# Another order of work in the projections of an attention and fp4 feed-forward layer

## The reference

```python
q, k, v = (split_heads(einsum('bsh,oh->bso', x, w) * s + b) for w, s, b in ...)   # 16 heads of 16
attn = softmax(einsum('bhqd,bhkd->bhqk', q, k) / 4)
x = layernorm(x + (einsum('bhqk,bhkd->bhqd', attn, v) -> [b,s,256]) @ w_o.T * s_o + b_o)
gate, y = fp4(x) @ fp4(w_gate).T, fp4(x) @ fp4(w_up).T       # 704 wide
h = silu(gate) * y
out = layernorm(x + fp4(h) @ fp4(w_down).T)
```

## Time and profile before

| | |
|---|---|
| median of 3 runs | 2128.46 us |
| profiled execution, own time | 2129.26 us |
| its span | 2127.5 us |
| TensorE / VectorE / ScalarE / GpSimd busy | 96% / 89% / 79% / 38% |
| projections (0 to 233 us): TensorE / VectorE / ScalarE busy | 198.9 / 145.1 / 125.8 us |
| attention (233 to 1560 us): TensorE / VectorE / ScalarE busy | 1291.1 / 1231.3 / 1150.0 us |
| feed-forward (1560 to 2128 us): TensorE / VectorE / ScalarE busy | 554.6 / 524.1 / 396.9 us |

### The profile page before, as it was taken

One profiled execution on the slowest core, in us unless ns is written; L12 is line 12 of the kernel. 1 busy time (PEld: TensorE's weight loads), 2 busy tenths in 40 slices (PEclk: granted clock), 3 DMA queues, 4 the chain that ended last, 5 costly groups with the idle time before them and its releaser, 6 DMA issues.

```text
span 2127.5 us, 42069 instructions
## 1 busy us (share of the span) xinstructions
PE 2044.5 (96%) x15836; PEld 1061.2 (50%) x15836; DVE 1900.4 (89%) x2497; ACT 1672.7 (79%) x3246; POOL 800.2 (38%) x712
## 2 busy tenths in 40 slices
PE   8798999999999999999999999999989999999998
PEld 6566533333333333333333333333367777777776
DVE  4676799999999999999999999998189999999996
ACT  6454788888888888888888888888857777777775
POOL 3000299999400000000000000000068888888885
PEclk9899899999999999999999999999999999999999
DMA  6864723323322422422432332330121122211210
GB/s 214 213 225 162 179 43 65 55 47 60 59 48 53 67 47 44 76 47 43 72 52 43 69 56 43 60 60 18 51 76 60 60 60 60 60 60 60 60 31 20
DMA packets 106615, 153.09 MB, mean 72 GB/s; under 512 B 22124, under 2 KB 68972, under 8 KB 106412
## 3 DMA queue, kind: packets, MB, share of 16 engines
q1 hardware_dynamic: 98732, 142.79, 29.9%
q10 hardware_dynamic: 7392, 7.34, 1.1%
q0 software_dynamic: 288, 0.27, 0.1%
HBM read 89.53 MB, written 59.24 MB: 70 GB/s over the span
## 4 chain that ended last, share of the span: by engine, by line
PE 77%; DVE 10%; ACT 3%; issue 1%; POOL 0%; POOLq 0%; DVEq 0%
PE ps L815 25%; PE ps L863 23%; PE ps L1128 12%; DVE negmax L968 9%; PE ps L1150 8%; PE ps L1117 3%; PE ps L1139 2%; ACT craw L927 2%; PE ps L835 2%; PE ps L1158 1%; PE ps L478 1%; PE ps L488 0%; DVE halfmax L561 0%; DVE vals L606 0%; ACT parts L550 0%
## 5 line engine op out<-in xcount | busy, mean ns | idle before, releaser
L919 ACT ACTIVATE room<-ps 128x512 f32<-128x512 f32 x2048 | 1105.2, 598 | 150.6 <-PE ps L835 120.1
L968 DVE TENSOR_REDUCE negmax<-ps 128x1 f32<-128x1024 f32 x984 | 1189.3, 1221 | 36.4 <-PE ps L815 30.8
L835 PE MATMUL ps<-qs,ks 50*128 50x512 f32 x2048 | 756.7, 450 | 3.1 <-DVE vals L606 2.4
L815 PE MATMUL ps<-ks,qs 48*128 48x512 f32 x1968 | 721.1, 446 | 16.5 <-DVE negmax L968 16.5
L863 PE MATMUL ps<-room,vals 128*17 128x256 f32 x8192 | 642.9, 386 | 9.2 <-ACT craw L927 0.2
L815 PEld LDWEIGHTS ps<-ks,qs 48*128 48x128 f32 x1968 | 291.6, 185 | 428.1 <-DVE negmax L968 316.0
L1373 POOL TENSOR_TENSOR ctxT<-cin 128x256 f32<-128x256 f32 x64 | 58.8, 918 | 971.0 <-DMA cin<-rden 971.0
L863 PEld LDWEIGHTS ps<-room,vals 128*17 128x17 f32 x8192 | 138.1, 95 | 378.5 <-issue 216.3
L835 PEld LDWEIGHTS ps<-qs,ks 50*128 50x128 f32 x2048 | 308.2, 185 | 22.4 <-ACT room L919 16.2
L1128 PE MATMUL ps<-wguT,xqT 128*128 128x512 f32 (+1 forms) x1152 | 266.0, 385 | 2.1 <-DVE xqT L1301 2.1
L1128 PEld LDWEIGHTS ps<-wguT,xqT 128*128 128x128 f32 x1152 | 210.1, 189 | 58.7 <-issue 20.2
(11 more groups left out here) (109 smaller groups left out, 2213.6 us busy)
## 6 DMA issues: line engine op xcount, KB each, us to landing
qk_parts<-parts SPq DMA_DIRECT2D x64, 512.0 KB, 2.8
qs<-qk_parts SPq DMA_DIRECT2D x192, 128.0 KB, 4.4
ks<-qk_parts SPq DMA_DIRECT2D x192, 128.0 KB, 7.1
ctx_raw<-craw SPq DMA_DIRECT2D x64, 256.0 KB
cin<-ctx_raw SPq DMA_DIRECT2D x64, 128.0 KB
cin<-rden SPq DMA_DIRECT2D x64, 128.0 KB
xin<-in_L_attn_x_dram SPq DMA_DIRECT2D x32, 256.0 KB, 4.7
out_dram<-fin SPq DMA_DIRECT2D x64, 128.0 KB, 1.7
```

Source lines behind the costliest of these rows:

```text
L815: return nc.tensor.matmul(ps[:, MX + 2 * (item[i.k, u] % 2) + bank, :], qs[rows, i.slot(RING), pair, t * P:(t + 1) * P], ks[rows, i.slot(R ...
L835: nc.tensor.matmul(ps[:, score_bank(i, s * GH + n), :], ks[rows, slot, pair, kt * P:(kt + 1) * P], qs[rows, slot, pair, qh * BANK:(qh + 1) ...
L919: nc.scalar.activation(prob[:, prob_slot(i, s), SCORE_ORDER[n], :], ps[:, score_bank(i, s * GH + n), :], ACT.Exp, scale=float(D) ** -0.5). ...
L968: nc.vector.tensor_reduce(negmax[:, j.slot(RING), max_column(u):max_column(u) + 1], ps[:, bank:bank + 2, :], AX.XY, ALU.max, negate=True). ...
```

## The change

In `project`, TensorE, VectorE and SyncE get another order, some waits are narrowed, and a few waits at the start of `attend` are replaced by later ones. No arithmetic is added or taken away. ScalarE follows TensorE: in chunk 0 it waits for the query constants alone, copies weight 1 (keys) between A0 and A1, weight 2 (values) and x of chunk 1 between A1 and A2, and waits for the key constants before A2; in chunk 1 it copies weight 3 first. VectorE splits x of chunk 1 between S1 and its first values. Weight m was transposed into bank 2 + m before. Cut to its core:

```diff
+    def w_bank(m):
+        return (MX, MX + 1, VV, MX)[m]
     def units(i):
-        if i.k < MAX_FROM:
-            return []
         first = (i.k - MAX_FROM) * MAX_PER
-        return range(first, min(first + MAX_PER, MU + LEAD))
+        if i.k < MAX_FROM:
+            return [None] * MAX_PER
+        if i.k < TURN:
+            return list(range(first, first + MAX_PER))
+        return [u if MU <= u < MU + LEAD else None for u in range(first - 1, first - 1 + MAX_PER)]
     def scale_job(i):
-        return {MAX_FROM - 2: 0, MAX_FROM - 1: 1, NCH - 2: 2}.get(i.k)
+        return {0: 0, 2: 1, NCH - 3: 2}.get(i.k)
@@ project, sync @@
-            group = {MAX_FROM - 2: 0, MAX_FROM: 1}.get(i.k)
+            group = {MAX_FROM - 2: 0, MAX_FROM + 1: 1}.get(i.k)
         for i in chunks():
+            first_groups(i)
             stage_weights(scale_job(i))
...
-            first_groups(i)
@@ project, tensor @@
         pe.wait_ge(ident_ready, 1)
         weights_by_input(0)
         transpose_x(At(None, 0, 2))
-        for m in range(1, 4):
-            weights_by_input(m)
-        pe.wait_ge(wT_ready, 4)
-        pe.wait_ge(w_split, 2)
         for i in chunks():
-            if i.plus(1).ok(NCH):
+            if i.k == 1:
+                weights_by_input(3)
+            if 0 < i.k < NCH - 1:
                 transpose_x(i.plus(1))
+            if i.k == 0:
+                pe.wait_ge(w_split, 1)
+            pe.wait_ge(xT_ready, i.lin(1, 1))
+            queries_and_keys(i, 0)
             if i.k == TURN:
                 pe.wait_ge(max_whole, 1)
                 maxima_out.transpose(nc, ps[:, MX], negmax, ident, At(None, 0, RING))
-            pe.wait_ge(xT_ready, i.lin(1, 1))
-            queries_and_keys(i, 0)
             max_unit(i, 0)
-            values(i, 0)
-            queries_and_keys(i, 1)
+            if i.k == 0:
+                weights_by_input(1)
+                queries_and_keys(i, 1)
+                weights_by_input(2)
+                transpose_x(i.plus(1))
+                pe.wait_ge(wT_ready, 3)
+                pe.wait_ge(w_split, 2)
+                values(i, 0)
+            else:
+                values(i, 0)
+                queries_and_keys(i, 1)
+            max_unit(i, 1)
             values(i, 1)
-            max_unit(i, 1)
             queries_and_keys(i, 2)
+            max_unit(i, 2)
             values(i, 2)
-            max_unit(i, 2)
             queries_and_keys(i, 3)
+            max_unit(i, 3)
             values(i, 3)
-            max_unit(i, 3)
+        pe.wait_ge(max_whole, 2)
@@ project, vector @@
         for i in chunks():
-            if i.plus(1).ok(NCH):
+            if i.k == TURN:
+                maxima_out.split(nc, dve, ps[:, MX], At(None, 0, RING), first_maxima)
+            take_max(i, 0)
+            if 0 < i.k < NCH - 1:
                 split_x(i.plus(1))
-            if i.k == TURN:
-                whole_max(0, S // P, MU)
-                maxima_out.split(nc, dve, ps[:, MX], At(None, 0, RING), first_maxima)
             split_qk(i, 0)
-            take_max(i, 0)
+            if i.k == 0:
+                split_weights(1)
+            take_max(i, 1)
             split_qk(i, 1)
...
             values(i, 0)
-            take_max(i, 1)
-            split_qk(i, 2)
             take_max(i, 2)
+            split_qk(i, 2)
+            take_max(i, 3)
+            if i.k == TURN - 1:
+                whole_max(0, S // P, MU)
+            if i.k == NCH - 2:
+                whole_max(1, LEAD // GH, MU + LEAD)
             split_qk(i, 3)
             values(i, 1)
-            take_max(i, 3)
-            weight_scales(scale_job(i))
-        whole_max(1, LEAD // GH, MU + LEAD)
+            weight_scales(scale_job(i.plus(-1)))
@@ attend, tensor @@
         pe.wait_ge(first_maxima, 1)
-        pe.wait_ge(qk_float, 4 * (T // BANK))
-        pe.wait_ge(v_ready, 2 * (T // BANK))
@@ attend, tensor, score_tile @@
+            if i.k == 0 and s * GH + n < SRING:
+                pe.wait_ge(qk_float, 4 * (T // BANK) - 1 + n % 2)
+                pe.wait_ge(v_ready, 2 * (T // BANK) - 1)
@@ attend, tensor, values @@
+                if i.k == 0 and s == 0:
+                    pe.wait_ge(v_ready, 2 * (T // BANK))
```

More of the change, by code:

```diff
@@ L208, in build @@
         weights_in = [sem(f"weights_in{j}") for j in range(4)]
-        qk_consts_in = sem("qk_consts_in")
+        qk_consts_in = [sem(f"qk_consts_in{j}") for j in range(2)]
         vo_consts_in = sem("vo_consts_in")
@@ L424, in weights_by_input @@
             pe.wait_ge(weights_in[m], 16)
+            if m == 3:
+                pe.wait_ge(w_split, 1)
             for c in range(HC):
                 for o in range(HC):
-                    last = nc.tensor.transpose(ps[:, 2 + m, c * H + o * P:c * H + (o + 1) * P],
+                    last = nc.tensor.transpose(ps[:, w_bank(m), c * H + o * P:c * H + (o + 1) * P],
                                                w_nat[:, m, o, c * P:(c + 1) * P], ident[:, :])
@@ L439, in transpose_x @@
             last.then_inc(xT_psum, 1)
-        pe.wait_ge(ident_ready, 1)
-        weights_by_input(0)
-        transpose_x(At(None, 0, 2))
-        for m in range(1, 4):
-            weights_by_input(m)
-        pe.wait_ge(wT_ready, 4)
-        pe.wait_ge(w_split, 2)
         def max_unit(i, k):
-            if k >= len(units(i)):
+            u = units(i)[k]
+            if u is None:
                 return
-            u = units(i)[k]
             group, t, pair, bank = unit_at(u)
@@ L529, in copy_weights, with copy_qk @@
             dst = wqk[:, 0, m] if m < 2 else wT[:, m - 2]
-            nc.scalar.activation(dst, ps[:, 2 + m, :].rearrange("p (c o) -> p c o", c=HC),
+            nc.scalar.activation(dst, ps[:, w_bank(m), :].rearrange("p (c o) -> p c o", c=HC),
                                  ACT.Copy).then_inc(wT_ready, 1)
+        def copy_qk(i, m):
+            act.wait_ge(qk_psum, i.lin(4, m + 1))
+            wait(act, qk_split, i.lin(4, m - 1))
+            nc.scalar.activation(qf[:, m % 2], ps[:, QK + m % 2, :], ACT.Identity,
+                                 bias=b_col[:, m // 2, m % 2:m % 2 + 1],
+                                 scale=s_all[:, m // 2:m // 2 + 1])
+            nc.scalar.activation(parts[:, i.slot(2), m, 0], ps[:, QK + m % 2, :], ACT.Identity,
+                                 bias=b_col[:, m // 2, m % 2:m % 2 + 1],
+                                 scale=s_all[:, m // 2:m // 2 + 1]).then_inc(qk_float, 1)
@@ L533, in scalar @@
         copy_weights(0)
         copy_xT(At(None, 0, 2))
-        for m in range(1, 4):
-            copy_weights(m)
-        act.wait_ge(qk_consts_in, 64)
         for i in chunks():
-            if i.plus(1).ok(NCH):
+            if i.k == 1:
+                copy_weights(3)
+            if 0 < i.k < NCH - 1:
                 copy_xT(i.plus(1))
             wait(act, qk_stored[i.slot(2)], i.turn(2, 64))
[L543 to L552, removed]
+            if i.k == 0:
+                act.wait_ge(qk_consts_in[0], 32)
@@ L554, in vector @@
+            copy_qk(i, 0)
+            if i.k == 0:
+                copy_weights(1)
+            copy_qk(i, 1)
+            if i.k == 0:
+                copy_weights(2)
+                copy_xT(i.plus(1))
+                act.wait_ge(qk_consts_in[1], 32)
+            copy_qk(i, 2)
+            copy_qk(i, 3)
     def vector(dve):
         def take_max(i, k):
-            if k < len(units(i)):
-                u = units(i)[k]
+            u = units(i)[k]
+            if u is not None:
                 group, t, pair, bank = unit_at(u)
```

32 lines of the change are left out of this document (20 added, 12 removed).

## The result

The changed kernel takes 2101.66 us (median of 4 runs, 2099.8 to 2104.07), the kernel before 2129.31 (4 runs, one more than in the first section): ratio 0.9875, 95% interval 0.9853 to 0.9898. The profiled execution took 2099.8 us, 29.5 less than that of before, and its span is 29.6 shorter. The forecast was 2093. The time is 8.7 us above it: inside the range of 2085 to 2106, and outside the 2088 to 2098 that the forecast gave to its own case.

What follows compares the result with a forecast made beforehand. The prediction took TensorE's waits before 250 us to decide the time; savings of 3.0 + 10.6 + 7.1 + 6.7 + 1.2 - 0.6 + 2.5 + 5.0 = 35.5 us off 2129.3, less 0.8 for the median, gave 2093 us, range 2085 to 2106.

Steps and rivals of the forecast that it cites:

- its own case: Whole kernel: clock kept and chunk 4 as summed, 2093 us, range 2088 to 2098, chance 0.5.
- Chunks with maxima, 7.1 us: Chunks 5 to 11: maxima ahead of splits leave no wait, 12.4 us a chunk against 13.41, 7.1 us off.
- Chunk 12, 6.7: Chunk 12: earlier combining and later transposition of the maxima, 11.9 us against 18.64, 6.7 us off.
- chunk 13, 1.2: Chunk 13: goes from 13.60 to 12.4 us, 1.2 us off.
- chunk 14, -0.6: Chunk 14: gets one unit of maxima, 0.6 us on.
- Start, 3.0: Before chunk 1: QK0 needs only the first weight and x, so chunk 1 starts at 24.5 us; 3.0 us off.
- Hand-over, 2.5: Projection to attention: first score follows the last V at once, first exp follows A3; 2.5 us off.
- Clock, 5.0: Start of attention: without the 2.39 us gap TensorE's clock does not fall to 0.50; 5.0 us off.
- the rival, given 0.2: Start of attention: the clock falls at the hand-over anyway, without the 5 us, 2098 us; chance 0.2.
- Chunk 4, 10.6: Chunk 4: earlier loads and weight cut it from 27.34 to 16.7 us, 10.6 us off.
- late in chunk 4: Chunk 4: weight or stacks still come late, 23.8 us and not 16.7, kernel 2100, with the clock 2105; chance 0.15.

Runs made afterwards that it cites:

- weight first: Changed kernel with chunk 2's feed-forward weight issued ahead of the twelve stack loads, not behind them: 2099.6 us, ratio 0.9867 to the kernel before.
- loads behind the stores: Changed kernel with the stack loads issued behind chunk 2's stores, the weight ahead of both: 2096.7 us, ratio 0.9859 to the kernel before.
- early weight: Changed kernel with the second feed-forward weight loaded in chunk 1 and its scales made at chunk 2's end: 2100.7 us, ratio 0.9868 to the kernel before.
- wait by piece: Changed kernel with each copy waiting only for its own piece's store two chunks earlier, not all four: 2102.1 us, ratio 0.9875 to the kernel before.
- old turn: Changed kernel with group 0's maxima again combined at chunk 12's start and transposed ahead of QK0: 2108.8 us, ratio 0.9908 to the kernel before.
- old hand-over: Changed kernel with the old waits for all copies and values before attention's first score: 2103.9 us, ratio 0.9876 to the kernel before.

## Why the prediction was right, and where it missed

- **Chunks with maxima, 7.1 us:** right. 12.40 us a chunk, no M waiting for TM; undoing it gave 13.41. That one M costs 0.64 us and not what its columns take was read from unblocked rows and held.
- **Chunk 12, 6.7; chunk 13, 1.2; chunk 14, -0.6:** right: 6.75, 1.25, and 1.9 us from chunk 14's opening to the first score where 2.5 - 0.6 was forecast.
- **Start, 3.0:** 2.7; against the 24.10 to 25.54 us at which chunk 1 opened in all kernels with the new start, 2.5 to 3.9.
- **Hand-over, 2.5:** right; its 2.5 less the 0.6 for chunk 14 are the 1.9 above.
- **Clock, 5.0:** 5.2 in the profiled execution, which has partly to be called luck: the rival, given 0.2, came about in five of ten traces with this hand-over, at a loss of 0 to 10 us. The profiled execution, with its clock kept, missed 2093.8 by 6.0, the median missed 2093 by 8.7. That the rest comes from runs with a lower clock is likely and not shown.
- **Chunk 4, 10.6:** the step that failed, by its size: 4.7. The forecast had 12.4 + 3.1 + 1.2 = 16.7 us and it took 22.62, which is 5.9 of the 6.0 us. Three terms were too small. The stop for the weight and its scales was 5.4 us and not 3.1. The stop for the stores of chunk 2, priced at 0 to 1 us and summed at nothing, was 1.4. The slow matmuls behind the stops cost 3.4 and not 1.2.
- **Why these two transfers came late.** The weight took 13.4 us to its use, as the 13.6 of the row; but it was issued at 47.67 and not at 46.0, and the forecast had taken the middle between this row and a guess of 10. The last store of chunk 2 was taken to be issued at 47.5 and to land by 61. It was issued at 52.1, as the loads began at 42.2 instead of 39.3 and as SyncE's own issues slowed behind the loads: those four stores took 0.47, 2.09, 1.33 and 1.28 us to issue instead of 0.36. It then took 16.2 us to land. The loads began late because the last store of chunk 1 landed in 5.3 us and not in the median 2.8; the same store took 5.5 before the change, so the trace of before could have told this.
- **Small slips in the working.** 34.9 + 1.4 + 2.8 is 39.1 and not 39.3, and 45.6 + 8.4 is 54.0 and not 54.4. The five steps of 2.14 us on VectorE begin at 238.31; from 240.45 to 249.00 there are four. None of them changes the sum by more than 0.4 us.
- **The ring-order rule** of the Trainium skill ("DMA: Bandwidth & Descriptors", Queues, rings and completion order), that descriptors are consumed in ring order, was weighed and given no price. The same sentence of that page adds that a later descriptor may finish its write before an earlier one, so "can't pass" and "land after" in the prediction are more than it says. What was waited for agrees with the order: in the two kernels with the weight first, putting the loads behind the stores instead of ahead of them turned ScalarE's wait of 8.7 us for the stores into none, and M0's wait for the stacks from 2.66 into 6.14 us. The runs don't tell the ring's order from the order in which SyncE issues.
- The rival "late in chunk 4" (23.8 us, 2100 for the kernel) was the nearest to the truth, at 0.15. That the time is in the range is owed to the room which that rival and the one on the clock had made, not to the forecast's own case.

## What to carry to other kernels

Where the profile shows DMAs full, the time from issue to landing is only half of the forecast. Work out when each transfer can be issued as well: what its queue waits for, how long the same transfer took to land at that place in the trace of before and not in the median, and that issues behind many loads can slow. In the four stores of chunk 2, 4.6 us of the miss lay in the issue and 2.6 in the landing. Several waits on one bottleneck give their gain only when all are taken away together (the early weight 3.1 us and the wait by piece 0.2 alone, 7.7 together). A gain that rests on the clock staying up is worth its price times the share of executions in which it does.

## What the runs showed of the hardware

- From 44 to 52 us, while the loads of 128 KB into 16 partitions, a load of x and the weight were under way, the DMAs were fully busy (share 1.04 to 1.09) and moved 161 to 170 GB/s in the changed kernel. In three kernels with the same queue up to there (wait by piece, old turn, old hand-over) they moved only 120 to 131, at a share of 1.02 to 1.08. The cause of that difference is open. Once mostly 512 KB stores from 128 partitions were left, they moved 393 to 404 at a share of 1.05 to 1.07.
- Behind the twelve loads and the weight, with the DMAs full, SyncE took up to 3.1 us to issue a 512 KB store (median 2.1 of seven, from 48 to 60 us), where it had taken 0.36 before. Full DMAs alone are not the cause: with the loads behind the stores, six stores from 44 to 57 us took 0.36 to 0.52 us to issue at a DMA share of 1.02 to 1.10.
- Between 20 and 260 us, a stop of 2.3 to 2.8 us on TensorE was followed by the lower clock in six cases (2.39, 2.60 and 2.63 us at the hand-over; 2.29, 2.66 and 2.77 in chunk 4) and not in two (2.42 and 2.50 in chunk 4).
- With the new hand-over, where no stop was longer than 0.3 us, a fall behind the thin stretch lasted from 3 to 20 us, with TensorE's busy share at 100% all the while. Whether it fell differed between kernels with the same instructions there.
